# A gated linear-attention layer with a channel-mix layer: second phase reordered across tiles, weight loads moved to GpSimd's queue

## What is computed

```python
q, k, v = heads(x @ Wq) * scale, heads(x @ Wk), heads(x @ Wv)
gk = heads(log_sigmoid(x @ gk_w1 @ gk_w2 + gk_b2) / 16)
S = S * exp(g_t)[..., None] + k_t[..., None] * v_t[..., None, :]   # scan
o_t = einsum('bhk,bhkv->bhv', q_t, S)
g = (x @ Wg).reshape(B, L, N_HEADS, DV)
rms = o * rsqrt(mean(o * o, axis=-1, keepdims=True) + EPS)
o = rms * g_norm_w * (g * sigmoid(g))
x = layernorm(x + o.reshape(B, L, 2048) @ Wo)
x_prev = shift(x)                                  # one token back
xr, xk = mu_r * x + (1 - mu_r) * x_prev, mu_k * x + (1 - mu_k) * x_prev
x = layernorm(x + sigmoid(xr @ W_r.T) * (square(relu(xk @ W_k.T)) @ W_v.T))
```

## Time and profile before

| | us |
|---|---|
| median of 2 runs | 2345.56 |
| the two runs | 2327.14, 2363.99 |
| the profiled execution | 2329.61 |
| its span on the slowest core (core 7) | 2328.1 |
| spans of the 8 cores | 2310.1 to 2328.1 |
| busy in it: TensorE matmuls / VectorE / ScalarE / GpSimd | 1730.3 / 1312.6 / 477.9 / 48.1 |

### The profile page before, as it was taken

One profiled execution on the slowest core, in us unless ns is written; L12 is line 12 of the kernel. 1 busy time (PEld: TensorE's weight loads), 2 busy tenths in 40 slices (PEclk: granted clock), 3 DMA queues, 4 the chain that ended last, 5 costly groups with the idle time before them and its releaser, 6 DMA issues.

```text
span 2328.1 us, 31040 instructions; the slowest of 8 cores (2310.1 to 2328.1 us)
## 1 busy us (share of the span) xinstructions
PE 1730.3 (74%) x11392; PEld 1084.1 (47%) x11392; DVE 1312.6 (56%) x2837; ACT 477.9 (21%) x563; POOL 48.1 (2%) x65
## 2 busy tenths in 40 slices
PE   0388888888888888883777786887764777778775
PEld 0155555555555555552444554454442444444442
DVE  0154444454444444443566666665666488877776
ACT  0132333223332323331110101001101111122210
POOL 0000000000000000000000000000000000000000
PEclk9999999999999999997898898777987899999997
DMA  6885441110111111004542333323313221121210
GB/s 96 104 110 91 64 64 28 28 27 12 27 28 28 28 28 26 21 19 112 169 109 64 110 81 93 97 64 93 98 55 109 91 73 56 72 73 73 73 73 37
DMA packets 128840, 157.34 MB, mean 68 GB/s; under 512 B 4321, under 2 KB 102626, under 8 KB 128242
## 3 DMA queue, kind: packets, MB, share of 16 engines
q0 software_dynamic: 42784, 56.76, 15.5%
q1 hardware_dynamic: 85906, 98.59, 12.9%
HBM read 144.98 MB, written 65.01 MB: 90 GB/s over the span
## 4 chain that ended last, share of the span: by engine, by line
PE 54%; DVE 27%; issue 8%; DMA 6%; ACT 3%; DVEq 1%; ACTq 0%; SPq 0%; POOLq 0%
PE PO L606 9%; PE PBIG L574 7%; PE PBIG L325 7%; PE PBIG L358 5%; PE PBIG L768 5%; PE PO L374 5%; PE PO L756 3%; PE PO L471 3%; DVE F L340 3%; PE PBIG L453 2%; PE PO L478 2%; DVE F L631 2%; DVE F L625 2%; DVE B L774 2%; DVE F L793 2%
## 5 line engine op out<-in xcount | busy, mean ns | idle before, releaser
L574 PE MATMUL PBIG<-B,arena 128*128 128x256 bf16 x2048 | 276.5, 306 | 160.6 <-ACT F L581 122.4
L574 PEld LDWEIGHTS PBIG<-B,arena 128*128 128x128 bf16 x2048 | 222.6, 109 | 215.3 <-issue 165.8
L606 PE MATMUL PO<-arena,O 128*128 128x512 bf16 x1024 | 241.1, 395 | 25.3 <-DVE F L614 25.1
L581 ACT ACTIVATE F<-PBIG 128x1024 f32<-128x1024 f32 x64 | 65.6, 1024 | 572.5 <-DVE Y L677 444.1
L332 DVE CAST V<-PBIG 128x512 bf16<-128x512 f32 x128 | 86.6, 687 | 168.8 <-PE PBIG L325 165.2
L606 PEld LDWEIGHTS PO<-arena,O 128*128 128x128 bf16 x1024 | 99.0, 101 | 161.1 <-issue 87.7
L585 DVE TENSOR_SCALAR V<-F,gnw_s 128x256 bf16<-128x256 f32 x256 | 73.4, 350 | 159.6 <-ACT F L581 159.6
L619 DVE SCALAR_TENSOR_TENSOR F<-PO,rstdA,F 128x1024 f32<-128x1024 f32 x96 | 123.2, 1284 | 53.2 <-PE PO L606 51.1
L325 PE MATMUL PBIG<-arena,B 128*128 128x512 bf16 x512 | 130.3, 422 | 10.8 <-ACT F L316 10.8
L325 PE MATMUL PBIG<-arena,B1u 128*128 128x512 bf16 x512 | 130.5, 423 | 9.8 <-ACT F L316 9.8
L471 PE MATMUL PO<-B 128*128 128x256 bf16 x512 | 101.2, 280 | 12.2 <-DVE PM L447 8.3
(11 more groups left out here) (130 smaller groups left out, 2612.0 us busy)
## 6 DMA issues: line engine op xcount, KB each, us to landing
orms<-O SPq DMA_DIRECT2D x16, 1024.0 KB
X<-x SPq DMA_DIRECT2D x16, 1024.0 KB
O<-orms SPq DMA_DIRECT2D x16, 1024.0 KB
ybuf<-Y SPq DMA_DIRECT2D x16, 1024.0 KB
Y<-ybuf POOLq DMA_DIRECT2D x16, 1024.0 KB, 5.4
out<-X SPq DMA_DIRECT2D x16, 1024.0 KB
B<-xt POOLq DMA_DIRECT2D x24, 512.0 KB, 8.2
arena<-wv POOLq DMA_DIRECT2D x1, 4096.0 KB, 29.1
```

The lines of the kernel that those rows point to most:

```text
L574: fns.append(lambda E, m=m, mm=mm, kc=kc, b0=b0, xfm=xfm: E.matmul(PBIG[:, b0 * 512 + mm * 256:b0 * 512 + (mm + 1) * 256], arena[:, A2_WG ...
L606: fns.append(lambda E, tb=tb, ng=ng, kc=kc, kk=kk, p=po: E.matmul(p[:, ng * 512:(ng + 1) * 512], ot[:, kc * 256 + tb * 128:kc * 256 + tb * ...
```

## The change

It has three parts.

**Queue of the weights.** arena_load_r issues on gpsimd instead of sync, for A2's two loads and B's three.

**Buffer of the silu.** It writes F2 instead of F1, and the multiplies read F2.

**Order of the tiles.** emit_a2_tile becomes three functions: a2_mid(i), the four quarters; a2_wo_group(i, obh, j), one Wo group and its eviction; a2_tail(i, obh), groups 6 and 7 and the tail of step 4. The loop puts a2_mid(i) first, then a2_tail(i-1), then load_a2(i+1), then groups 0 to 5 of tile i. The last tile's tail stands behind the loop.

```diff
-            S.group("sync", [lambda E, d=dst, s_=src_ap: E.dma_start(out=d, in_=s_)],
+            S.group("gpsimd", [lambda E, d=dst, s_=src_ap: E.dma_start(out=d, in_=s_)],
                     reads=[rbuf], writes=[wbuf], dma=True)
...
-        def emit_a2_tile(i):
+        def a2_mid(i):
             t0 = i * T
...
-            if i + 1 < NT:
-                load_a2(i + 1)
...
                 S.group("scalar", [lambda E, qtr=qtr, b0=b0: E.activation(
-                    F1t[:, (qtr % 2) * 1024:(qtr % 2) * 1024 + 1024],
+                    F2t[:, (qtr % 2) * 1024:(qtr % 2) * 1024 + 1024],
                     PBIG[:, b0 * 512:(b0 + 2) * 512], AF.Silu)],
-                    reads=[bPB[b0], bPB[b0 + 1]], writes=[bF1])
+                    reads=[bPB[b0], bPB[b0 + 1]], writes=[bF2])
...
-                S.group("vector", fns, reads=[bF1, bCONST], writes=[bV1q[qtr]])
+                S.group("vector", fns, reads=[bF2, bCONST], writes=[bV1q[qtr]])
...
+            return obh
+
+        def a2_wo_group(i, obh, j):
+            tb, h = j // 4, j % 4
+            ot = Ot[i % 2]
+            po, pob = POt[j % 2], bPO[j % 2]
...
+        def a2_tail(i, obh):
+            t0 = i * T
+            xb, xt = bX[i % 2], Xt[i % 2]
+            for j in (6, 7):
+                a2_wo_group(i, obh, j)
             a2_obh[i % 2] = obh
...
+            pend = None
             for i in range(NT):
-                emit_a2_tile(i)
+                obh = a2_mid(i)
+                if pend is not None:
+                    a2_tail(*pend)
+                if i + 1 < NT:
+                    load_a2(i + 1)
+                for j in range(6):
+                    a2_wo_group(i, obh, j)
+                pend = (i, obh)
+            a2_tail(*pend)
```

More of the change, by code:

```diff
@@ L581, in emit_a2_tile @@
                 S.group("scalar", [lambda E, qtr=qtr, b0=b0: E.activation(
-                    F1t[:, (qtr % 2) * 1024:(qtr % 2) * 1024 + 1024],
+                    F2t[:, (qtr % 2) * 1024:(qtr % 2) * 1024 + 1024],
                     PBIG[:, b0 * 512:(b0 + 2) * 512], AF.Silu)],
-                    reads=[bPB[b0], bPB[b0 + 1]], writes=[bF1])
+                    reads=[bPB[b0], bPB[b0 + 1]], writes=[bF2])
                 fns = [lambda E, mm=mm, qtr=qtr: E.tensor_scalar(
                     V1t[:, qtr * 1024 + mm * 256:qtr * 1024 + (mm + 1) * 256],
-                    F1t[:, (qtr % 2) * 1024 + mm * 256:(qtr % 2) * 1024 + (mm + 1) * 256],
+                    F2t[:, (qtr % 2) * 1024 + mm * 256:(qtr % 2) * 1024 + (mm + 1) * 256],
                     gnw4[:, (qtr * 4 + mm) % 4:(qtr * 4 + mm) % 4 + 1], None,
                     ALU.mult) for mm in range(4)]
-                S.group("vector", fns, reads=[bF1, bCONST], writes=[bV1q[qtr]])
+                S.group("vector", fns, reads=[bF2, bCONST], writes=[bV1q[qtr]])
                 if qtr % 2 == 1:
@@ L597, in emit_a2_tile @@
                         reads=[bV1q[2 * kh], bV1q[2 * kh + 1], ob], writes=[obh[kh]])
[L598 to L622, removed]
@@ new lines, in a2_mid @@
+            return obh
[3 more added lines that the diff above has]
+            po, pob = POt[j % 2], bPO[j % 2]
+            fns = []
+            for ng in range(2):
+                for kk in range(4):
+                    kc = 4 * h + kk
+                    fns.append(lambda E, tb=tb, ng=ng, kc=kc, kk=kk, p=po: E.matmul(
+                        p[:, ng * 512:(ng + 1) * 512],
+                        ot[:, kc * 256 + tb * 128:kc * 256 + tb * 128 + 128],
+                        arena[:, A2_WO + kc * 1024 + ng * 512:A2_WO + kc * 1024 + ng * 512 + 512],
+                        start=(kk == 0), stop=(kk == 3)))
+            S.group("tensor", fns, reads=[bARH, obh[h // 2]], writes=[pob])
+            rc = rstdA[:, i * 8 + h * 2 + tb:i * 8 + h * 2 + tb + 1]
+            if h == 0:
+                S.group("vector", [lambda E, tb=tb, p=po, rc=rc: E.tensor_scalar(
+                    F1t[:, tb * 1024:(tb + 1) * 1024], p[:, :], rc, None,
+                    ALU.mult)], reads=[pob, bRS], writes=[bF1])
+            else:
+                S.group("vector", [lambda E, tb=tb, p=po, rc=rc:
+                                   E.scalar_tensor_tensor(
+                    F1t[:, tb * 1024:(tb + 1) * 1024], p[:, :], rc,
+                    F1t[:, tb * 1024:(tb + 1) * 1024], ALU.mult, ALU.add)],
+                    reads=[pob, bRS], writes=[bF1])
```

## The result

The changed kernel takes 2340.65 us (median of 16 runs), the kernel before beside it 2329.99 (15 runs). The ratio is 1.0047, 95% interval 1.0035 to 1.0058: 11 us slower, within the 2% that counts as no change, and still clear of noise. Some executions of either kernel take up to 190 us longer, at a lower granted clock on one die: medians here are over all runs, ratios leave those out. The forecast was 2351, 21 us or 0.9% above the profiled execution of before. The profiled execution after has a span of 2335.1 us on core 7, 7.0 more than before.

What follows compares the result with a forecast made beforehand. Bound: in A2 TensorE waits behind silu, which waits for the previous tile's normalisation. Some 14 us gained at the start, about 22 at the end and 57 lost by the order gave about 2351 us; range 2330 to 2385.

Steps and rivals of the forecast that it cites:

- The new loop: A2's tile loop: period 44.3 us, 3.4 longer than before; the wait is moved, not removed, as eviction 0 stands behind the tail.
- pause 11.9: A2, each tile: TensorE idles 11.9 us until eviction 0 starts behind the tail, more than the 8.41 that went.
- restart 2.6: A2, Wo groups 2 to 5: the clock falls in the pause, charged at 2.59 us a tile.
- The lower clock: A2 as a whole: the 14.3 us of lower clock and small stalls scale with matmul work to 17 us.
- rival 4: A2's lower clock: first half, it does not come, 17 us less, 2334 (10%); or it holds in every tile, 2399 (5%).
- The start: Start of A2: gate weights on POOL land at 1101, tile 1 starts at about 1130, 14 us earlier (bounds 5 and 20).
- The end: End of A2: B's weights just hidden, some 0.5 us left; about 22 us gained; phase B starts at 1835.8.
- rival 1: A2 after the pause: clock stays at 1.2 GHz for all four Wo groups, 66 us more, 2417; chance 8%.
- rival 2: A2's O load: comes late on SP, multiplies slip some 1.5 us, 2374; chance 8%.
- rival 3: A2's tail: hidden after all, VectorE's own work binds at about 31 us a tile, 200 us less, 2150; chance 3%.
- rival 5: A2's edges: give nothing as transfers share one set of engines, start 5 and end 15, 2367; chance 6%.

Runs made afterwards that it cites:

- the early loads: Changed kernel with A2's first X, O and xt loads ahead of A1's last tile, wo and wg right behind: 2303.04 us, ratio 0.9934 to the kernel before.
- f2_halves: Kernel before with silu in F2 and a separate dependency buffer for each half of F2: ratio 0.955 to the kernel before.

## Why the prediction was right, and by how much it was off

**The new loop: right.** The forecast period was 44.3 us; from 1311.03 the next gate part starts at 1355.42 in the same timeline, and from 1134.37 to 1754.47 lie 14 tiles of 44.29 us. Its steps: gate part 14.0 (measured 13.97 from start to start), eviction 6 3.88 us later (3.89), pause 11.9 (11.84 in most tiles), restart 2.6 (9.46 less 7.0 is 2.5). That the wait is moved and not removed is shown from two sides: its releaser is eviction 0, and it shrinks by what the tail is shortened. The run with the tail elsewhere on VectorE, where it is gone, agrees, though that run changed more.

**The lower clock: a term of 17 us that was not there.** This is the largest mis-sized term. The step said that the 14.3 us of lower clock and small stalls scale to 17. After, 14 x 44.29 leaves no room for it beside the 15 periods: from tile 1's gate to the last group 6, at 1754.47 + 44.5 or about 1799.0, are 664.6 us, and 664.5 + 17 were forecast. No long stretch at 0.81 was in that execution, nor is there one in that of the queue alone, which has TensorE's order of before and a period of 40.89 us over 14 tiles, where 586.65 us for 14 make 41.90. So the order of before does not bring the stretch by itself. The forecast took what one execution had for a property of the kernel, and the execution it compared with was some 10 us slower than the kernel before is in the experiments. The first half of rival 4, given 10%, named the outcome (2334, for a profiled execution of 2336.66), but gave TensorE's idle time as the cause: that is not borne out, since the same order without the stretch has the same idle time.

**The start: 14 us forecast, 9.7 in the span.** The gate started where it was said (1101 against 1101.46). Group 0 waited 4.91 us for the Wo weights where a microsecond or two was said, and A1 had ended 2.0 us later in that execution (last small matmuls at 1075.09 against 1073.10 of before). Tile 1 started at 1134.37 instead of 1130.

**The end: right.** Tail 17.9 us after the last group 6 starts, operand 5.9 later, and the first product when it was ready. wk landed some 2 us before the operand, where 1 was reckoned, so the 0.5 us taken for it was not paid on this core. That the cover is thin showed in three experiments, where wk came after the operand: by 2.2 us with the early loads, 5.2 with the shorter tail, 13.5 with the tail moved. Phase B then took 512.1 us, and 513.3 before.

The sum by these: 2349.1 forecast for the span, plus 4.4 at the start, less 17 for the clock, less 0.5 for wk and less 1.2 in phase B, is 2334.8, and 2335.1 was measured. Three of these four corrections lower the sum and one raises it, so the 14 us between the forecast span and the measured one are what is left after a small part has cancelled.

**The rivals.** The clock did not stay low longer after the longer pause (rival 1): the restart cost 2.5 us as before. The O load was not late (rival 2): no row of waits names it. The tail was not hidden (rival 3), though in the kernel with F2 in halves it is, at 33.9 us a tile; whether the 31 us of VectorE's work given there are a floor is not shown, since VectorE was busy for 27.2 of those 33.9 us. The edges did give something (rival 5): with the queue alone they are worth 34 us.

**Queue against queue.** The rule of the Trainium skill, "DMA: Bandwidth & Descriptors", "Issuing engine by pattern", that SyncE's queue is generally faster than GpSimd's, weighed in the prediction, is not seen as a loss here. In the early-loads kernel no load of X or O is issued beside wo and wg: from issue to landing wg takes 15.0 us and wo 16.4, against 15.4 for wg on SP. The 18.6 us from which the prediction took a slower POOL were of wq, a load that reads f32 and writes bf16. The 20.8 us of wg in the changed kernel I put down to sharing with X and O. Moving the loads out of SP's row to POOL is worth 34 us; no run put them early on SP, so place and issuer are told apart only by these loads' times.

## What to carry to other kernels

When one engine's long tail holds another up, ask first what the waiting engine can do beside it, and count that cover in microseconds: here 64 gate matmuls (7.0 us) plus a buffer conflict were traded for two Wo groups (3.5 us) with a buffer limit of two, and the loss was the difference. A false dependency (two halves of one buffer under one name) is looked for before the order is rewritten: the buffer edit that was a few lines of this change, done in halves and without the reorder, makes the kernel 4.5% faster. Loads for the next phase belong on a queue whose head is free early; the rows of these loads speak for the place in the queue, and not for the engine that issues them. And one execution's slow stretch is no property of the kernel: look at a second execution before it goes into a sum.

## What was not expected of the hardware

The cost of a restart varied without following the length of the pause, and between tiles with the same pause. With the queue alone, the 64 matmuls (7.15 us at full clock) behind the ten pauses of 8.40 and 8.41 us took from 8.64 to 9.61 us, so 1.5 to 2.5 lost. In the single tiles shown above it was about 2.5 us after 8.4 and 12.2 us of idling, 1.8 after 6.3 (8.92 for 64), 1.5 after 9.7, and 1.6 after 4.7 (5.23 for 32 that take 3.65). In f2_halves, with a pause of only 4.16 us, the clock was full in the pause and fell behind it. Its windows (stretch, us, busy by engine, granted clock, DMA share, GB/s):

```profile
1261.00:1265.00 4.00, 0.00 (x0) 0.00 (x0) 3.83 (x11) 2.05 (x2) 0.87 (x1) 1.00 0.73 255
1265.10:1267.10 2.00, 2.00 (x6) 0.72 (x7) 1.96 (x8) 0.00 (x0) 0.00 (x0) 0.53 0.76 71
1267.10:1269.10 2.00, 2.00 (x7) 0.79 (x6) 1.64 (x2) 0.00 (x0) 0.00 (x0) 0.61 1.10 114
1269.10:1273.00 3.90, 3.90 (x20) 1.69 (x18) 2.84 (x3) 0.00 (x0) 0.00 (x0) 1.00 0.98 215
```

So a short pause costs too, after it is over. What decided the stretch at 0.81 in the kernel before stays open: it was in one execution, and no experiment was made for it. Two cores of each die had it and the other two had not: from 1430 to 1600 us cores 0, 1, 6 and 7 were granted 0.76 to 0.77 on average, cores 2 to 5 at the same time 0.88.
